# Vision tower, attention scores: four heads per product, masked halves copied apart, extremes taken in the same pass

## The reference

```python
qkv = x2 @ _fq_weight_int8(w_qkv).T + b_qkv               # 12 heads of 16 features
attn = jnp.einsum('bhnd,bhmd->bhnm', q, k) * scale        # 16 x 16 per image and head
attn, s_attn = _fq_act_uint4(attn)                        # one minimum and one maximum over all of attn
attn = _int_log2_softmax(attn, s_attn)                    # integer softmax along m
x = jnp.einsum('bhnm,bhmd->bhnd', attn, v)
x, _ = _fq_act_uint4(x)                                   # again over the whole tensor
x = x @ _fq_weight_int8(w_proj).T + b_proj
x, _ = _fq_act_uint4(x)                                   # and again
```

## Time and profile before

| | us |
|---|---|
| median of 3 runs | 640.88 |
| lowest, highest | 640.64, 645.03 |
| profiled execution | 637.5 |
| span of its trace, first to last instruction | 635.7 |
| PE busy / DVE busy / ACT busy | 508.8 / 329.8 / 197.3 |

### The profile page before, as it was taken

How to read it: one execution, slowest core, us unless ns; L and a number is a source line. 1 busy time by engine, 2 the same in 40 slices (tenths; PEclk the granted TensorE clock), 3 DMA queues, 4 the chain that set the end, 5 groups by cost and what they waited for, 6 DMA issues and landing times.

```text
span 635.7 us, 13176 instructions
## 1 busy us (share of the span) xinstructions
PE 508.8 (80%) x4722; PEld 468.8 (74%) x4723; DVE 329.8 (52%) x1032; ACT 197.3 (31%) x430; POOL 143.5 (23%) x148
## 2 busy tenths in 40 slices
PE   4999998858805447489999779935999999999960
PEld 4999994558704347479999666824899999999960
DVE  1678999447999985512222382866122222222206
ACT  4520124325793345033334242231212211122110
POOL 1690000000001000424431200003344444443220
PEclk9999999965657756689999985955999999999995
DMA  8980000000004002396558520014965666567216
GB/s 318 412 307 16 1 2 0 0 6 2 0 0 174 3 0 101 85 278 187 164 153 332 170 77 2 1 51 149 283 189 157 191 204 188 161 179 195 65 44 279
DMA packets 35382, 81.46 MB, mean 128 GB/s; under 512 B 7142, under 2 KB 18242, under 8 KB 34306
## 3 DMA queue, kind: packets, MB, share of 16 engines
q1 hardware_dynamic: 29762, 69.37, 33.7%
q0 software_dynamic: 5568, 11.41, 6.6%
HBM read 70.33 MB, written 10.42 MB: 127 GB/s over the span
## 4 chain that ended last, share of the span: by engine, by line
PE 70%; DVE 15%; ACT 5%; DMA 4%; issue 3%; SPq 2%; ACTq 0%; POOL 0%; DVEq 0%; POOLq 0%
PE ps L1091 18%; PE ps L845 13%; PE ps L1067 12%; PE ps L1075 6%; PE ps L960 2%; DMA arena<-ffn_b 2%; DVE h L1851 2%; PE ps L929 2%; PE ps L930 2%; PE ps L826 2%; PE ps L825 1%; PE ps L785 1%; DVE xT L1695 1%; DVE arena L1565 1%; PE ps L1058 1%
## 5 line engine op out<-in xcount | busy, mean ns | idle before, releaser
L1091 PE MATMUL ps<-arena,xn 128*128 x696 | 123.2, 328 | 4.1 <-ACT xn L735 3.3
L1091 PEld LDWEIGHTS ps<-arena,xn 128*128 128x128 f32 x696 | 111.8, 190 | 6.4 <-issue 6.2
L482 POOL DMA_INDIRECT xT<-rows,from_i x58 | 56.0, 966 | 191.9 <-DVE from_i L1709 136.6
L1067 PE MATMUL ps<-xn,arena 128*128 128x128 f32 x696 | 91.3, 283 | 2.0 <-DMA arena<-ffn_b 1.9
L845 PE MATMUL ps<-arena 128*128 128x192 f32 (+1 forms) x588 | 85.4, 336 | 9.0 <-ACT arena L521 9.0
L1067 PEld LDWEIGHTS ps<-xn,arena 128*128 128x128 f32 x696 | 88.6, 199 | 3.6 <-DMA arena<-ffn_b 3.5
L845 PEld LDWEIGHTS ps<-arena 128*128 128x128 f32 (+1 forms) x588 | 83.9, 197 | 9.2 <-ACT arena L521 8.7
L1734 DVE COPY xn<-ps 128x128 f32<-128x128 f32 x58 | 16.9, 292 | 125.9 <-PE ps L1059 125.9
L495 POOL DMA_INDIRECT made<-xT,to_i x58 | 57.0, 983 | 110.2 <-DVE xT L1746 66.4
L738 ACT ACTIVATE xn<-ps 128x384 f32<-128x384 f32 x78 | 32.7, 493 | 125.9 <-PE ps L1077 99.9
L735 ACT ACTIVATE xn<-ps,b_all 128x128 f32<-128x128 f32 x114 | 30.8, 390 | 46.9 <-PE ps L1077 35.0
(11 more groups left out here) (364 smaller groups left out, 806.4 us busy)
## 6 DMA issues: line engine op xcount, KB each, us to landing
arena<-ffn_a SPq DMA_DIRECT2D x58, 384.0 KB, 4.0
arena<-ffn_b SPq DMA_DIRECT2D x116, 96.0 KB, 4.3
arena<-x_blocks SPq DMA_DIRECT2D x16, 384.0 KB, 7.0
arena<-x_strips SPq DMA_DIRECT2D x3, 1536.0 KB, 11.9
...
```

Source lines behind the costliest of these rows:

```text
L482: pool.indirect_dma_start(sx[:, k % 6], None, F["src"], bass.IndirectOffsetOnAxis(from_i[:, k:k + 1], 0)).then_inc(sem(f"sx_in{k % 6}"), 16)
L1067: pe.matmul(ps[:, up_bank(u, c // 3), 128 * (c % 3):128 * (c % 3) + 128], w_up[:, u, 128 * c:128 * c + 128], sT[:, u, 0:128], start=(c % 3 ...
L1091: mm = pe.matmul(ps[:, result_bank(k, N), 0:DIM], hT[:, u % 2, 128 * c:128 * c + 128], F["w2"][:, bass.ds(e2 + DIM * c, DIM)], start=(c == ...
```

## The change

- **Products.** `scores` on PE uses 64 partitions (four heads) and 128 columns of keys per product: three products per block of 32 rows instead of six, 192 in all. Each g fills three banks (0 to 2 or 4 to 6) instead of four.
- **Keys.** Four masks (one per head of four, `key_mask`, made by four small DVE instructions before `affine(0)`) take the place of two. ACT makes the four masked copies of `mt` 1 for all g. DVE makes those of `mt` 2 for all g, in eight instructions of 64 partitions x 256 elements (even and odd pairs of images go to separate halves of the partitions). ACT copies the queries of `mt` 2 in two halves.
- **Order.** The last g makes its parts in the order 2, 1, 0 (`QK_PARTS`). `values(0, 2)` no longer stands before the scores; `values(0, 3)` stands behind them and ahead of the spread, `values(3, 8)` behind it. ACT copies values 0 to 3 after the scores.
- **Halves.** ACT copies both halves of a quarter, each times its mask, in one instruction each, into `S` and `S_odd`. DVE adds them from SBUF with `tensor_tensor_reduce`, which keeps a running minimum; L1465 is gone. PE waits for ACT (`s_act`) instead of DVE before reusing banks.
- **First half of the output.** ACT copies it into SBUF (`o_first`) while DVE reduces the second half; DVE rounds it from there.
- **Projection.** DVE scales each bank with `tensor_tensor_reduce` and a running maximum; the four L1620 are gone, and the minimum is taken twice (10 and 6 token rows) instead of four times.

```diff
-V_BANKS = (4, 5, 2, 3, 5, 6, 7, 4)
+QK_PARTS = ((0, 1, 2), (0, 1, 2), (0, 1, 2), (2, 1, 0))
+V_BANKS = (3, 7, 2, 3, 5, 6, 7, 4)
...
-        kk0 = view(0, [64, 64]); kk1 = view(4096, [64, 64])
+        kk0 = view(0, [64, 128]); kk1 = view(26880, [32, 128])
         q0 = view(8192, [TOKS]); q1 = view(10240, [TOKS])
-        S = view(12288, [16, HEADS * 16])
+        S = view(12288, [16, HEADS * 16]); S_odd = view(18432, [16, HEADS * 16])
...
-                if mt == 1:
-                    src = src.rearrange("p (a m t) -> p a m t", m=2, t=4)
-                    act.activation(of_keys(kk0, 0, i), src, ACT.Copy, scale=mask_ke)
-                    ins = act.activation(of_keys(kk0, 1, i), src, ACT.Copy, scale=mask_ko)
+                if mt == 0:
+                    ins = act.activation(of_row(q0, i), src.rearrange("p (b t) -> p b t", t=4), ACT.Copy)
+                elif mt == 1:
+                    for x in range(4):
+                        ins = act.activation(of_keys(kk0, x, i), src.rearrange("p (x a t) -> p x a t", a=2, t=4), ACT.Copy,
+                                             scale=key_mask[x])
                 else:
-                    ins = act.activation(of_row((q1 if mt else q0)[parts], i), src.rearrange("p (b t) -> p b t", t=4), ACT.Copy)
+                    for odd in range(2):
+                        ins = act.activation(of_pairs(q1[64 * odd:64 * odd + 64], odd)[:, :, :, 4 * i:4 * i + 4], of_pairs(src, odd), ACT.Copy)
                 ins.then_inc(sem("qk_act"), 1)
...
                 act.wait_ge(sem("s_ps"), g + 1)
-                for r in range(4):
-                    w = 16 * len(BANK_HEADS[r])
-                    ins = act.activation(S[:, 4 * g:4 * g + 4, 16 * HEAD_AT[r]:16 * HEAD_AT[r] + w],
-                                         ps[:, 4 * (g % 2) + r, 0:4 * w].rearrange("p (t c) -> p t c", t=4), ACT.Copy, scale=mask_a)
+                src = ps[:, 4 * (g % 2):4 * (g % 2) + 3, :].rearrange("p r (a t c) -> p a t r c", a=2, t=4)
+                for odd, (dst, mask) in enumerate(((S, mask_a), (S_odd, mask_b))):
+                    ins = act.activation(dst[:, 4 * g:4 * g + 4, :].rearrange("p t (r c) -> p t r c", r=3), src[:, odd], ACT.Copy, scale=mask)
                 ins.then_inc(sem("s_act"), 1)
...
             for g in (2, 3):
-                queries(g, 0)
-                queries(g, 2)
-            values(0, 2)
+                for mt in QK_PARTS[g]:
+                    queries(g, mt)
             for g in range(4):
                 scores(g)
-            values(2, 4)
+            values(0, 4)
             act.wait_ge(sem("wrow_in"), 1)
...
+            act.wait_ge(sem("o_read"), 1)
+            act.activation(o_first, half_ps[0], ACT.Copy).then_inc(sem("o_copied"), 1)
...
+                    if n in (3, 6):
+                        pe.wait_ge(sem("v_act"), n // 3)
                     if n >= 2:
-                        pe.wait_ge(sem("s_dve"), 3 if n < 4 else 4)
+                        pe.wait_ge(sem("s_act"), 3 if n < 4 else 4)
...
-                if g == 1:
-                    pe.wait_ge(sem("v_act"), 2)
                 if g >= 2:
-                    pe.wait_ge(sem("s_dve"), g - 1)
+                    pe.wait_ge(sem("s_act"), g - 1)
                 for tl in range(4):
                     for j in range(4):
                         col = 128 * (4 * g + tl) + 32 * j
-                        for chunk in range(2):
-                            for r in range(4 if chunk == 0 else 2):
-                                rows = slice(32 * r, 32 * r + 32)
-                                nh = len(BANK_HEADS[r])
-                                o = ps[32 * j:32 * j + 32, 4 * (g % 2) + r, 0:128 * nh].rearrange(
-                                    "p (a t s m) -> p a t s m", a=2, t=4, s=nh)[:, :, tl, 2 * chunk:2 * chunk + 2, :]
-                                mm = pe.matmul(o.rearrange("p a s m -> p s a m"), (q1 if chunk else q0)[rows, col:col + 32],
-                                               (kk1 if chunk else kk0)[rows, col // 32, :].rearrange("p (s a m) -> p s a m", s=2, a=2),
-                                               start=True, stop=True, skip_group_check=True)
+                        low, high, own = slice(0, 64), slice(64, 128), slice(64 * (j % 2), 64 * (j % 2) + 64)
+                        for r, (rows, q, k) in enumerate(((low, q0, kk0[:, col // 32]), (high, q0, kk0[:, col // 32]), (own, q1, kk1[:, col // 64]))):
+                            o = ps[32 * j:32 * j + 32, 4 * (g % 2) + r, :].rearrange("p (a t s m) -> p a t s m", a=2, t=4, s=4)[:, :, tl]
+                            mm = pe.matmul(o.rearrange("p a s m -> p s a m"), q[rows, col:col + 32],
+                                           k[rows].rearrange("p (s a m) -> p s a m", s=4, a=2), start=True, stop=True, skip_group_check=True)
                 mm.then_inc(sem("s_ps"), 1)
...
-            values(0, 2)
             for g in range(4):
                 scores(g)
-            values(2, 4)
+            values(0, 3)
             spread(0, 0, 1)
-            values(4, 8)
+            values(3, 8)
 
...
-                src = qk_ps(n, parts).rearrange("p (a m t) -> p a m t", m=2, t=4)
-                kk = kk1[0:64] if mt == 2 else kk0
-                dve.tensor_scalar(of_keys(kk, 0, i), src, mask_ke[parts], None, ALU.mult)
-                dve.tensor_scalar(of_keys(kk, 1, i), src, mask_ko[parts], None, ALU.mult).then_inc(sem("k_dve"), 1)
+                src = qk_ps(n, parts)
+                for odd in range(2):
+                    for x in range(4):
+                        ins = dve.tensor_scalar(of_keys(kk1[64 * odd:64 * odd + 64], x, i), of_pairs(src, odd), key_mask[x][parts], None, ALU.mult)
+                ins.then_inc(sem("k_dve"), 1)
...
-                for r in range(4):
-                    w = 16 * len(BANK_HEADS[r])
-                    sv = S[:, 4 * g:4 * g + 4, 16 * HEAD_AT[r]:16 * HEAD_AT[r] + w]
-                    ins = dve.scalar_tensor_tensor(
-                        sv, ps[:, 4 * (g % 2) + r, 4 * w:8 * w].rearrange("p (t c) -> p t c", t=4), mask_b, sv, ALU.mult, ALU.add)
-                ins.then_inc(sem("s_dve"), 1)
+                quarter = slice(768 * g, 768 * g + 768)
+                even, odd = (x.rearrange("p t c -> p (t c)")[:, quarter] for x in (S, S_odd))
+                dve.tensor_tensor_reduce(even, even, odd, 1.0, 3e38, ALU.add, ALU.min,
+                                         stat[:, 256 + g:257 + g]).then_inc(sem("s_dve"), 1)
                 dve.wait_ge(sem("s_dve"), g + 1)
-                dve.tensor_reduce(rmax[:, 48 * g:48 * g + 48], S[:, 4 * g:4 * g + 4, :].rearrange("p t (s m) -> p (t s) m", m=16),
-                                  AX.X, ALU.max)
-                link(dve.tensor_reduce(stat[:, 256 + g:257 + g], S[:, 4 * g:4 * g + 4, :], AX.XY, ALU.min, negate=True))
+                ins = dve.tensor_reduce(rmax[:, 48 * g:48 * g + 48], S[:, 4 * g:4 * g + 4, :].rearrange("p t (s m) -> p (t s) m", m=16),
+                                        AX.X, ALU.max)
+                if g == 3:
+                    link(ins)
...
+            dve.wait_ge(sem("o_copied"), 1)
             for tq in range(2):
-                ins = dve.tensor_scalar(o1_of(tq), o_of(tq).rearrange("p (h j d) -> p h j d", h=HEADS, j=4), ninv, ROUND, ALU.mult, ALU.add)
+                ins = dve.tensor_scalar(o1_of(tq), o_first[:, 768 * tq:768 * tq + 768].rearrange("p (h j d) -> p h j d", h=HEADS, j=4), ninv, ROUND, ALU.mult, ALU.add)
...
-                ins = dve.tensor_tensor(pp[:, 2 * b:2 * b + 2, :], ps[:, b, 0:2 * DIM].rearrange("p (a c) -> p a c", a=2),
-                                        pbc[:, 0:1, :].to_broadcast([128, 2, DIM]), ALU.mult)
-                if b % 2:
+                ins = dve.tensor_tensor_reduce(pp[:, 2 * b:2 * b + 2, :], ps[:, b, 0:2 * DIM].rearrange("p (a c) -> p a c", a=2),
+                                               pbc[:, 0:1, :].to_broadcast([128, 2, DIM]), 1.0, -3e38, ALU.mult, ALU.max,
+                                               stat[:, 232 + b:233 + b])
+                if b in (4, 7):
                     link(ins)
-                    four = pp[:, 2 * b - 2:2 * b + 2, :]
-                    dve.tensor_reduce(stat[:, 240 + b // 2:241 + b // 2], four, AX.XY, ALU.max)
-                    ins = dve.tensor_reduce(stat[:, 256 + b // 2:257 + b // 2], four, AX.XY, ALU.min, negate=True)
+                    part = (pp[:, 0:10], pp[:, 10:16])[b // 7]
+                    ins = dve.tensor_reduce(stat[:, 256 + b // 7:257 + b // 7], part, AX.XY, ALU.min, negate=True)
             link(ins)
-            level_scalars(2, stat[:, 240:244], 4, 6, 7)
+            level_scalars(2, stat[:, 232:240], 2, 6, 7)
```

38 lines of the change are left out of this document (21 added, 17 removed).

## The result

Four runs of the changed kernel give 624.38 us (619.99 to 627.90), four of the kernel before beside them 641.95 (640.64 to 645.03). The ratio is 0.973, 95% interval 0.968 to 0.979. With all later runs of the same two kernels (21 and 62 in all) the medians are 625.6 and 640.7 us, 15.1 apart; resampling those runs gives 14.1 to 17.0. Four slow runs are left out, one of the changed kernel at 672.9 us, with a granted clock of 0.77 where its others have 0.86 to 0.89, and three of the kernel before at 645.1 to 646.7, over 1.5% above its fastest.

A forecast was written before the change was run, and what follows sets the result against it. Outside the unchanged expert layers, engines wait for each other, with PE waiting for instruction blocks in the scores. Savings of 0.5 + 8.5 + 0.85 + 2.5 = 12.35 us off the 640.88 median gave 628.5 us, range 625 to 638.5.

The forecast's parts named there:

- The products: 8.5 us less: Score products on PE: 384 pairs instead of 768 at 28.8 ns, without gaps, ending at 137.8 instead of 146.85.
- 6.4 ns are fixed: Score products: of an old pair's 12.0 ns at full clock, 6.4 do not go with the array's clock, 5.6 do.
- I take the array part times four: Score products: twice the columns and twice the rows give 28.8 ns per pair at full clock, 51 at half.
- the fetch binds: Score products, bound: if only columns count, a pair costs 17.6 ns and instruction fetch sets three blocks of 3.5, 10.4 us.
- Gaps: PE's five gaps in the scores, 7.8 us, are waits for the next 128-pair instruction block, whose fetch takes about 3.5 us.
- Start: Ahead of the scores: they begin at 126.5 (125.5 to 127.8) instead of 127.03, 0.5 us earlier.
- scores that start after 128, with ACT or DVE as the releaser: Start of the scores: one of the signs named in advance that would show the forecast wrong.
- Scores to spread: From the scores' end to the spread: ACT's copies 1.63, accumulator reading 0.15, one minimum gone; 4.35 instead of 5.2, 0.85 less.
- Output: Rounding of the output's first half: no gain, since PE's transposes wait for ACT's half too.
- Projection: DVE's scaling and reducing of the projection: 8.7 us instead of 11.2, 2.5 less.
- The first rival: Scores: the clock falls to half at 133 as before, 2.7 less there, 635.7 us in all; chance 0.2.
- the slow one: Scores: 64-row products queue for their rows at half clock, over 52 ns per pair; 7.7 more, 648.6 us; chance 0.09.

The follow-up runs named there:

- a_half_columns: Changed kernel with every score product cut to two heads, 64 columns instead of 128; 8.4 us from first to last product, against 8.9 to 9.4.
- a_products_twice: Changed kernel with every score product issued twice in a row to the same place, 768 pairs; 39.9 ns per pair, no gaps.
- a_no_o_first: Changed kernel without ACT's copy of the output's first half, DVE rounding from PSUM as before; 625.2 us (623.9 to 626.1, 6 runs).
- a_control2: Changed kernel, unchanged, run again as a control; 625.6 us (621.0 to 629.0, 5 runs).
- a_filled_wait2: Changed kernel with 20 idle transposes on PE during its wait for `xn`; 623.1 us (619.9 to 624.7, 6 runs), ratio to the kernel before 0.970.
- a_control: Changed kernel, unchanged, run again as a control; 627.1 us (622.1 to 629.7, 6 runs).

## Where the forecast held, and the step that failed

**The sum.** 12.35 us were named up to the third spread; measured between profiles with like starts (the table) it is 14.8: 0.1 at the start, 10.45 products, 1.05 from the last product to the first spread, 0.3 to the second, 2.9 to the third. The term that was mis-sized is "The products: 8.5 us less", by 1.95 of the 2.45.

- **Products.** First to last product takes 19.5 before and 8.9 to 9.4 after (up to 9.8 at full clock in variants with the same products). The step that failed is "6.4 ns are fixed" with "I take the array part times four", 28.8 ns per pair at full clock and 51 at half. Measured are 18.8 in the first burst, up to 21.4 later, and 35 at half clock, almost twice: nearly all of a wide pair goes with the array's clock. The old one goes from 10.4 (starts within the bursts of the earlier trace rows) to 15.2, so not all of it does; I read that as a second limit which it meets at full clock, and the sum had added two limits of which the larger counts. At half clock the factor between the two pairs is 35 / 15.2 = 2.3, of which the columns are 35 / 18.8 = 1.9 and the rows 18.8 / 15.2 = 1.2 (a_half_columns). The Trainium skill's page "TensorEngine Tiling (Array Packing)", Available Configurations, lists 16 tiles of 32x32 and 8 of 64x32. With twice the columns I had made a factor of four of that; the measurement decides. The case of the lower bound, "the fetch binds", is the one that came and should have been the one taken, and its 10.4 us was too high as well: "three blocks of 3.5" counts the last block whole. The time is that of the periods and then of what is left, five periods of 3.6 and 105 pairs in 1.6 us before, two of 3.7 and 89 pairs in 1.9 us in the first profile after. "A block of 128 pairs then takes 3.7 us" came out right for the wrong reason.
- **Gaps.** Right: the instruction blocks. Half of the products, twice the products and half of the columns all keep breaks every 128 pairs, 3.4 to 3.9 apart. "Mostly hidden" (the Trainium skill, "Runtime: NRT & Kernel Launch", Instruction fetch mechanics) becomes truer as pairs get dearer: 1.3 to 2.2 of each 3.5 to 3.7 us are lost with old pairs at 10 to 15 ns, 0.2 to 0.9 (once 1.3) with wide pairs at 19 to 21, nothing at the 39.9 of a_products_twice.
- **Start.** Named 126.5, measured 126.8 to 128.0 at full clock and 128.6 to 131.2 with the fall: nothing gained instead of 0.5. A sign named for being wrong came with it, "scores that start after 128, with ACT or DVE as the releaser" (129.29, DVE). DVE's g took 3.4, not 3.1. I had not seen that ACT's longer copies lengthen PE's wait for `xn` from 2.1 to 2.6; whether that makes a fall of the clock likelier is open.
- **Scores to spread.** Last product to spread: 5.5 before, 4.5 after, 1.0 less where 0.85 was named. The copies 1.70 (1.63), the reading 0.08 (0.15). At full clock the values stayed hidden behind the work of ACT and DVE, as said.
- **First to second spread:** 0.3 less, not named. **Output:** 0, as named (a_no_o_first).
- **Projection.** Named 2.5, and 2.6 to 3.2 came; the minima took 2.15 and 1.35 and the stretch 8.0 instead of 8.7, since scaling with maximum has a step of 0.47 to 0.64 with its reading inside, where 0.65 was named.
- **The clock** stayed full through the scores in 12 of the 15 profiles with 64-row products, and was at half for some 3.4 us of them in three: from their start, behind PE's wait for the keys, in a_half_columns and a_control2, and from 1.2 us behind it in a_filled_wait2. In all four with the old products (gaps of 1.3 to 2.2) it fell between 131.9 and 135.9 and stayed low to their end. The first rival is out, and so is the slow one: 35 ns at half clock is under its 52.

**The range.** Of the 4.1 us between 628.5 and 624.4, 2.45 are these terms. Some 1.2 are the luck of four runs (625.6 in 21). The rest is below what these runs resolve. The range's lower end, 625.0, had products of 10.4 us in it, over 1 us more than came, and no scatter of the measurement itself, whose medians of four to six runs spread over 2.7 us. The 625.6 of 21 runs lies just inside, the 624.4 of the four just outside.

**What stays open:** why the last stretch scatters by 6 us with the same work (its half-clock phases lie differently in each trace), and how much of an earlier start arrives at the end: a_control2 began its scores 4.4 us after a_control and ended with the same span, 623.8.
